# Sums of x1 for the right side: from VectorE's accumulator to four ScalarE copies a chunk

## What is computed

```python
# first layer
n = layernorm(x, ln1)
left = sigmoid(n @ left1) * (n @ left2)
right = sigmoid(n @ right1) * (n @ right2)
p = layernorm(einsum('nsre,nkre->nske', left, right), ln2)
x1 = x + einsum('nrse,ez->nsrz', p, out_w) * sigmoid(n @ gate)
# second layer
left = x1 @ W_left + b_left + x1 @ W_eq + b_eq
right_sum = sum(x1 @ W_right + b_right, axis=2)
out = left * right_sum * sigmoid(x1 @ W_gate + b_gate)
result = layernorm(out @ W_out + b_out + x1)
```

## Time and profile before

| | us |
|---|---|
| Median of 3 runs (112.12 to 112.26) | 112.12 |
| Profiled execution, its own time | 112.37 |
| Span in the profile, first to last instruction | 110.6 |
| PE busy | 94.1 (85%) |
| PE weight loads busy | 73.9 (67%) |
| DVE busy | 75.8 (69%) |
| ACT busy | 66.4 (60%) |
| POOL busy | 62.3 (56%) |

### The profile page before, as it was taken

The page is one execution under the profiler, slowest core; times in us unless marked ns, Lnnn a source line. Parts: engine busy times, 40 slices in busy tenths (PEclk is TensorE's granted clock), DMA queues, the critical chain, the costliest instruction groups (busy, mean ns, idle before and its releaser), DMA issues. The chain is left out here.

```text
span 110.6 us, 1889 instructions
## 1 busy us (share of the span) xinstructions
PE 94.1 (85%) x600; PEld 73.9 (67%) x600; DVE 75.8 (69%) x284; ACT 66.4 (60%) x110; POOL 62.3 (56%) x78
## 2 busy tenths in 40 slices
PE   1997889999999899999979999999999996499100
PEld 1994568667787899354536789777887885399000
DVE  1474799957879500989957599699789954983500
ACT  0633987977774366885699445982896499221000
POOL 5059954999910310055289595587865491799300
PEclk9999999999999999999999999999999999959985
DMA  3999990000000000000000000000032006029996
GB/s 59 190 152 143 147 134 21 0 0 0 0 0 3 6 0 0 0 0 3 0 0 0 9 0 0 0 0 6 0 55 40 0 0 95 0 41 146 145 146 101
DMA packets 33546, 4.54 MB, mean 41 GB/s; under 512 B 33408, under 2 KB 33536, under 8 KB 33536
## 3 DMA queue, kind: packets, MB, share of 16 engines
q1 hardware_dynamic: 31776, 4.03, 29.7%
q10 hardware_dynamic: 1760, 0.38, 1.8%
HBM read 2.31 MB, written 2.10 MB: 40 GB/s over the span
## 5 line engine op out<-in xcount | busy, mean ns | idle before, releaser
L596 DVE TENSOR_TENSOR lr<-bank,sig_lr 128x512 f32<-128x512 f32 x16 | 15.9, 1043 | 3.9 <-ACT sig_lr L431 3.9
L817 PE MATMUL bank<-lr_blk,xnT 64*128 64x256 f32 x128 | 16.5, 392 | 1.2 <-ACT xnT L421 0.7
L354 POOL TENSOR_TENSOR t_tok<-p_sb,rstd 128x512 f32<-128x512 f32 x7 | 10.2, 1461 | 11.8 <-DVE rstd L666 11.8
L362 POOL TENSOR_TENSOR x_low<-x1T,x_high 128x512 fp32r<-128x512 f32 x8 | 10.3, 1293 | 7.5 <-ACT x_high L501 7.5
L817 PEld LDWEIGHTS bank<-lr_blk,xnT 64*128 64x128 f32 x128 | 11.7, 186 | 4.2 <-issue 2.1
L660 DVE BATCH_NORM_STATS2 stats<-p_sb 128x6 f32<-128x64 f32 x64 | 8.5, 213 | 7.0 <-ACT p_sb L465 7.0
L370 POOL TENSOR_TENSOR oT<-o_a,rsum 128x512 f32<-128x512 f32 x8 | 8.7, 1088 | 6.4 <-DVE o_a L706 4.3
L431 ACT ACTIVATE sig_lr<-bank 128x512 f32<-128x512 f32 x16 | 9.6, 598 | 3.7 <-PE bank L817 3.6
L978 PE MATMUL bank<-wout_blk,oT 128*128 128x128 f32 x64 | 9.4, 293 | 2.2 <-POOL oT L370 2.2
L978 PEld LDWEIGHTS bank<-wout_blk,oT 128*128 128x128 f32 x64 | 8.5, 201 | 4.0 <-POOL oT L370 3.2
L501 ACT ACTIVATE x_high<-x1T 128x512 fp32r<-128x512 f32 x8 | 5.0, 626 | 8.5 <-DVE x1T L697 8.4
(11 more groups left out here) (104 smaller groups left out, 202.3 us busy)
## 6 DMA issues: line engine op xcount, KB each, us to landing
x_tok<-in_x SPq DMA_DIRECT2D x14, 128.0 KB, 4.2
out<-sq SPq DMA_DIRECT2D x7, 256.0 KB, 3.4
x_tok<-in_x SPq DMA_DIRECT2D x3, 64.0 KB, 3.0
w_rep<-in_weights ACTq DMA_DIRECT2D x4, 45.1 KB, 3.1
out<-sq ACTq DMA_DIRECT2D x1, 128.0 KB, 4.0
out<-sq SPq DMA_DIRECT2D x1, 128.0 KB, 4.5
x_tok<-in_x ACTq DMA_DIRECT2D x1, 64.0 KB, 2.7
row_rep<-in_rows SPq DMA_DIRECT2D x1, 32.0 KB, 4.2
```

The source lines that it names most:

```text
L354: nc.gpsimd.tensor_tensor(place(t_tok[:, c % 2], 0, SPC), even_first(p_sb[:, :, s]), even_first(rstd[:, 1:2, s]).to_broadcast([P, 2, SPC / ...
L362: nc.gpsimd.tensor_tensor(x1_low[:, c % 2], x1T[:, c % 3], x1_high[:, c % 2], ALU.subtract).then_inc(x1_low_ready, 1)
L596: nc.vector.tensor_tensor(lr[:, :, s].rearrange("p f s -> p s f"), src[:, :, 2 * CH:4 * CH], sig_lr[:, j % 3].rearrange("p (s f) -> p s f" ...
L817: last = nc.tensor.matmul(dst, xnT[half, c, k * P:(k + 1) * P], lr_blk[half].rearrange("p g m c -> p g (m c)"), start=True, stop=True, ski ...
```

## The change

VectorE computes x1 of a chunk in one operation over all four blocks, without accumulator, and counts `x1_ready` up by four at its end. ScalarE gets a new step `sum_x1(c)`: four copies of one block each from `x1T` into a scratch tile `x1_seen` that nobody reads, whose accumulator output is the block's sum. They count a new semaphore, `x1_summed`. TensorE's `project_sums` waits for this one in place of `x1_ready`. VectorE, before it writes a buffer of `x1T` again, waits in addition until ScalarE has summed what was in it.

```diff
+            def sum_x1(c):
+                act.wait_ge(x1_ready, BLK * (c + 1))
+                if c:
+                    act.wait_ge(x1_summed, BLK * c)
+                for j in range(BLK):
+                    b = slice(j * P, (j + 1) * P)
+                    nc.scalar.activation(x1_seen[:, b], x1T[:, c % 3, b], ACT.Copy,
+                                         accum_out=x1_sum[:, c, j:j + 1]).then_inc(x1_summed, 1)
...
                 if 0 <= i - 2 < CHUNKS - 1:
                     gate1(i - 2)
+                if i == 2:
+                    sum_x1(0)
+                if 1 <= i - 1 < CHUNKS:
+                    sum_x1(i - 1)
                 if i == 2:
                     for c in range(4, CHUNKS):
                         gate0(c)
...
                 if c >= 3:
                     dve.wait_ge(y_ps, c - 2)
-                for j in range(BLK):
-                    b = slice(j * P, (j + 1) * P)
-                    nc.vector.scalar_tensor_tensor(out=x1T[:, c % 3, b], in0=bank[:, XT, b], scalar=vec("b_out"),
-                                                   in1=u[:, c % 2, b], op0=ALU.add, op1=ALU.add,
-                                                   accum_out=x1_sum[:, c, j:j + 1]).then_inc(x1_ready, 1)
+                    dve.wait_ge(x1_summed, BLK * (c - 2))
+                nc.vector.scalar_tensor_tensor(out=x1T[:, c % 3], in0=bank[:, XT], scalar=vec("b_out"),
+                                               in1=u[:, c % 2], op0=ALU.add, op1=ALU.add).then_inc(x1_ready, BLK)
...
             def project_sums(m):
-                pe.wait_ge(x1_ready, 2 * BLK * (m + 1))
+                pe.wait_ge(x1_summed, 2 * BLK * (m + 1))
```

More of the change, by code:

```diff
@@ L158, in pair_layers @@
         x1_sum = sb("x1_sum", [P, CHUNKS, BLK])
+        x1_seen = sb("x1_seen", [P, COLS])
         rsum = sb("rsum", [P, CHUNKS, BLK])
@@ L197, in pair_layers @@
         q_ps, xT_ps, x1_ready = sem("q_ps"), sem("xT_ps"), sem("x1_ready")
+        x1_summed = sem("x1_summed")
         rs_ps, rs_ready, l_ps, g1_ps, sig1_ready = (
```

## The result

The changed kernel is slower. Its median is 118.13 us against 112.12, the range of four runs 116.25 to 119.37 against 112.10 to 112.26. The ratio is 1.043 (95% interval 1.038 to 1.048), a smaller loss than the two medians give, because it leaves out two of the changed kernel's four runs, which took over 1.5% longer than its fastest.

What follows compares the result with a forecast made beforehand. GpSimd's `times_right(7)`, released by a ScalarE run, was taken to set the end. 112.37 + 6.07 for the copies + 1.3 for the clock = 119.7 us profiled, so median 119.5, range 115.5 to 122.3.

Steps and rivals of the forecast that it cites:

- (c): Iteration 6: S - 0.41 = 1.23 us more ahead of the table load, 0.45 hidden, TensorE 4.84 us later.
- Clock holds: Rival: S = 1.64 us without the clock term of (e), 118.2 us; chance 0.16.
- S: ScalarE's time for the four copies of a chunk, taken as 4 x 0.41 = 1.64 us, bounds 0.84 and 2.04.
- 5S - 2.13: Sum of the delays over iterations 2, 4, 6 and 8, without the clock: 6.07 us.
- (a): Iteration 2: copies of chunks 0 and 1 ahead of the gate sigmoids make TensorE 2S = 3.28 us later.
- VectorE's gain: x1 of a chunk whole 0.41 us earlier, counting only in iterations 6 and 8; 0.8 us with copies at no price.
- (e): TensorE's idle time of about 3 us in iteration 2 lowers its clock, adding 1.3 us (between 0 and 1.8).
- (b): Iteration 4: chunk 3's sums ahead of the table load; shift 3S - 0.86 = 4.06 us, including the earlier 3.28.
- (d): Iteration 8: chunk 7's sums in ScalarE's final run, ahead of the table load, add S - 0.41 = 1.23 us.
- free: Rival: the accumulator output costs nothing, S = 0.84 us, 2.11 in all, no clock fall, 114.2 us; chance 0.17.
- the chosen price: Each ScalarE copy brings a second instruction of 0.20 us, with 0.10 overlap: 0.41 us a copy, 1.64 a chunk.
- The free chunks: Odd iterations: all sums there fall in ScalarE's free time of 2.68 us, so they add nothing.

Runs made afterwards that it cites:

- the kernel with the gap filled: The changed kernel with ten idle matmuls on TensorE ahead of its wait in project_sums(0); ratio 1.038, median 116.32 us.
- the VectorE part alone: Against the kernel before: x1 in one VectorE operation, no sums at all and no ScalarE copies; ratio 0.991, median 111.23 us.

## Why the prediction was right, and where it was off

The path and the waits came true but for a part of (c); one term of the sum was mis-sized. The range of 115.5 to 122.3 was wide, and the single number nearest to the median of 118.13 is not the forecast of 119.5 but the 118.2 of the rival *Clock holds*. That is luck: it has a copy price that is too high and no clock term, and the profile shows a lower price and a clock that fell.

- *What bounds the kernel.* Right. `times_right(7)`, the row of five and the span all moved by 5.5, and the DMA share at the end is 0.96 as before.
- *The price.* S was 1.17, not 1.64, inside the bounds of 0.84 and 2.04. The step that failed is the term of 0.20 us for the second instruction: it lasts 0.19, but after its start the next copy waits only 0.09. I took the length of a whole one-column operation where half of the read is hidden behind the next copy. With 1.17 the sum's 5S - 2.13 is 3.72, 2.35 below the 6.07 forecast.
- *(a) The gap.* 2S is 2.34 with the measured S, and 2.21 were measured. ScalarE was 0.3 earlier (`gate1(0)` at 57.60, before at 57.92). Of that, 0.1 is there before any changed instruction (`evacuate_tT(2)` at 53.60 and 53.70), and 0.2 come from x1(0), which was whole sooner. Another 0.2 were lost between the copies of chunks 0 and 1, which start 0.48 apart in place of 0.29: the fifth waits for the last read of the fourth. "VectorE's gain is worth nothing here" was off by 0.2.
- *(e) The clock.* 1.3 taken, 1.35 measured in the profile (1.52 against the kernel with the gap filled), and the cause is shown by that kernel. The Trainium skill ("TensorE: Matmul & The Clock Gate", "What's actually happening") says that activity releases the throttle. The traces agree: the clock stayed at 1.00 where the gap was filled, and behind the gap it came back while TensorE worked (0.50 at 63, 1.00 at 66). The fall is not certain in every run: that at 116.25 seems to be without it, and there the rival *Clock holds* would be right on this term.
- *(b) Iteration 4.* 3S - 0.86 + 1.35 = 4.00 with the measured S and clock, 3.98 measured. That it fits to 0.02 is partly luck. TensorE's last pass was 3.49 late (70.25 for 66.76), 0.20 less than the terms give. `gate1(2)` then waited not for it, which would have made it start at 70.74, but for `high1(3)`, and started at 70.81. And the table load keeps 0.12 us from what stands ahead of it (before: 68.00 + 0.57 = 68.57, load at 68.69), which the sum left out.
- *(c) Iteration 6.* The load moved by 0.81 more, to 4.79, against S - 0.41 = 0.76. TensorE was 4.39 late at `project_y(4)`, so 0.40 were hidden, about the 0.45 of the sum. But the step took 4.39 as what goes on, and this failed: VectorE, which also waits for the root, carried the full 4.79 and ran without a pause to x1(7). Here are the changed kernel, and in the last row `scale3` of iteration 6 before:

```profile
85.34 0.35 DVE L731 RECIPROCAL rstd<-std 128x32 f32<-128x32 f32 x1 [2.00 <-ACT std L412]
...
86.66 1.04 POOL L372 TENSOR_TENSOR oT<-o_a,rsum 128x512 f32<-128x512 f32 x1 [2.13 <-issue]
87.14 1.10 DVE L745 TENSOR_TENSOR lr<-lr,rstd 128x512 f32<-128x512 f32 x1
...
90.84 0.75 DVE L712 SCALAR_TENSOR_TENSOR x1T<-bank,w_rep,u 128x512 f32<-128x512 f32 x1
...
82.73 0.73 DVE L731 TENSOR_TENSOR lr<-lr,rstd 128x512 f32<-128x512 f32 x1
```

  x1(7) starts 4.74 later than before although TensorE is 4.39 late, so 0.35 came back. The shorter x1(6) should have made VectorE 0.41 earlier here. But its `scale3` then started while GpSimd was in `times_right(4)` and lasted 1.10 us in place of 0.73, which took 0.37 of the 0.41 away again. (TensorE's `project_q(7)` was 4.50 late, 88.75 for 84.25, so that much would have stayed in any case.)
- *(d) Iteration 8.* `high1(7)` moved from 87.31 to 91.63, by 4.32, and S brings it to 5.49. `project_sums(3)` waited 0.67 us for its sums, without effect.
- *The whole.* 3.72 + 1.35 + 0.35 = 5.42, measured 5.51 between the two profiled executions. The forecast of 7.4 was 2.35 too high by the price of the read, and 0.4 too low by the clock and (c). The case that came true lies between "free" and the chosen price, with the clock term.
- *VectorE's gain.* 0.8 predicted, 1.0 measured, but from iterations 4 and 8, not from 6 and 8; 0.1 at the start can't be told from none. In iteration 6 it is hidden as long as TensorE keeps the pace, which gained 0.10 there. The size was right by luck.
- *The free chunks.* Right: chunks 2, 4 and 6 cost nothing that the time shows.

## What to carry to other kernels

Price an added operation by what stands behind it in its queue, not by the engine's busy share: four copies in the wrong place cost 0.8 us, net of VectorE's gain, and twelve in the right place none. Where an instruction writes a result that others wait for and one that is needed later, produce the first whole and early, even if the second then costs more on the same engine, where that engine has time behind it. When a step hides a delay on one engine, look for the others that wait for the same releaser, since the delay may go on through them. And when an operation comes earlier, look at what runs on the other engines at its new place: `scale3` came 0.4 us earlier and got 0.4 us longer.

## What the runs showed of the hardware

ScalarE's accumulator output is a second instruction of 190 ns, of which 0.09 us counts in the queue. On VectorE the read lasts 84 ns and starts together with the next operation (both at 53.47 in VectorE's timeline of before), and the four operations stay 0.27 us apart.

VectorE's `scale3` of 128x512 lasts 0.68 us by itself. In nine cases in the traces of before, the changed kernel and the VectorE part alone it started while GpSimd's `times_right` ran, and it then lasted 0.73 to 1.42 us and ended each time 0.54 to 0.55 us after GpSimd's operation. The reason was not tried.

A pause of 2.5 us in TensorE's work was followed by a stretch at 1.2 GHz that cost 1.35 us, and filling the pause avoided it. The length of the pause does not decide alone. Near the end of all twelve profiles TensorE waits 1.59 us for GpSimd. In six of them, that of before included, the granted clock was 0.50 soon after, and in the other six, that of the changed kernel included, it stayed at 1.00; there it cost no time: from before to the changed kernel `times_right(7)` and the span both moved by 5.5 us, with a low clock behind it in the one and a full one in the other.

In some executions of every kernel of this study but the one with the VectorE part alone, which ran only five times, there is a further loss of about 1.6 us. In the two profiles that hold it, the clock was at 0.50 at 38, behind a pause of half a microsecond. The same pause is in the profiles of before and of the changed kernel, where the clock stayed at 1.00. What decides whether it comes was not tried.
